# Row maxima one slot and a third ahead instead of two, with a new order of steps and a new prologue rotation

## What is computed

```python
q, k = _rope(q, k)
att = jnp.einsum('bhtd,bhsd->bhts', q, k) / math.sqrt(DH)
att = att + mask                       # causal
w = jax.nn.softmax(att, axis=-1)
y = jnp.einsum('bhts,bhsd->bhtd', w, v)
x = _layernorm(x + y @ W_o)
x = _layernorm(x + ffn(x))             # 8 experts, the best 2 of each token, 256 -> 256
```

## Time and profile before

| | us |
|---|---|
| median of three runs | 3246.15 |
| the profiled execution | 3247.9 |
| its span | 3246.2 |
| PE busy | 3110.3 (96%) |
| VectorE busy | 2684.6 (83%) |
| ACT busy | 1885.3 (58%) |
| GpSimd busy | 1198.2 (37%) |
| first score of attention | at 140.3 |
| the transpositions of x that begin each middle turn | 191.8 apart |
| last turn ends | at 3144.4 |

### The profile page before, as it was taken

How to read it: one execution, slowest core, us unless ns; L and a number is a source line. 1 busy time by engine, 2 the same in 40 slices (tenths; PEclk the granted TensorE clock), 3 DMA queues, 4 the chain that set the end, 5 groups by cost and what they waited for, 6 DMA issues and landing times.

```text
span 3246.2 us, 58552 instructions
## 1 busy us (share of the span) xinstructions
PE 3110.3 (96%) x18752; PEld 1712.3 (53%) x18752; DVE 2684.6 (83%) x8456; ACT 1885.3 (58%) x4257; POOL 1198.2 (37%) x1410
## 2 busy tenths in 40 slices
PE   4789999999999999999999999999999999999987
PEld 2234555555555555555555555555555555555555
DVE  6877888888888888888988888888888888888745
ACT  2266556575565656556575665657565565755551
POOL 3153424444243443424344342434324344442110
PEclk8699999999999999999999999999999999999997
DMA  5344324333442434334333442443443243344000
GB/s 134 62 70 81 60 57 77 62 68 66 80 65 50 78 58 79 60 76 65 55 73 61 83 65 57 73 66 68 66 83 60 55 79 61 69 65 70 4 27 14
DMA packets 174819, 210.95 MB, mean 65 GB/s; under 512 B 26008, under 2 KB 124592, under 8 KB 174256
## 3 DMA queue, kind: packets, MB, share of 16 engines
q1 hardware_dynamic: 173056, 202.98, 35.9%
q10 hardware_dynamic: 1456, 4.23, 0.3%
HBM read 138.44 MB, written 67.11 MB: 63 GB/s over the span
## 4 chain that ended last, share of the span: by engine, by line
PE 84%; DVE 8%; issue 3%; ACT 2%; POOL 1%; DMA 1%; ACTq 0%; SPq 0%; DVEq 0%; POOLq 0%
PE bank L917 22%; PE attend L1012 15%; PE scores L990 14%; PE bank L974 14%; PE bank L954 6%; PE bank L1036 3%; PE bank L963 3%; DVE bank L775 2%; PE bank L1020 1%; PE bank L942 1%; DVE maxima L778 1%; PE bank L1027 1%; PE bank L1044 1%; ACT weights L651 1%; PE bank L1068 1%
## 5 line engine op out<-in xcount | busy, mean ns | idle before, releaser
L651 ACT ACTIVATE weights<-scores 128x512 f32<-128x512 f32 (+3 forms) x3072 | 1333.5, 495 | 886.0 <-PE scores L990 872.7
L775 DVE CUSTOM_DVE_ANT_0 bank<-bank,far_q 128x128 f32<-128x128 f32 (+3 forms) x2048 | 963.1, 512 | 202.7 <-PE bank L974 187.2
L974 PE MATMUL bank<-k_stack,q_stack 96*128 96x512 bf16 (+3 forms) x3072 | 803.6, 333 | 31.7 <-DVE maxima L775 10.5
L990 PE MATMUL scores<-q_stack,k_stack 99*128 99x512 bf16 (+3 forms) x3072 | 821.1, 328 | 10.6 <-ACT weights L651 6.9
L571 POOL TENSOR_SCALAR_AFFINE_SELECT weights<-weights 128x512 f32<-128x512 f32 x512 | 325.4, 637 | 1269.4 <-ACT weights L651 1269.1
L778 DVE TENSOR_REDUCE maxima<-bank 128x1 f32<-128x512 f32 x1024 | 643.9, 682 | 71.2 <-PE bank L974 70.9
L1012 PE MATMUL attend<-weights,values 128*32 128x512 f32 (+3 forms) x6144 | 579.2, 492 | 1.0 <-POOL weights L571 0.9
L990 PEld LDWEIGHTS scores<-q_stack,k_stack 99*128 99x128 bf16 x3072 | 280.1, 97 | 411.8 <-ACT weights L651 154.6
L974 PEld LDWEIGHTS bank<-k_stack,q_stack 96*128 96x128 bf16 x3072 | 276.9, 98 | 400.6 <-issue 153.6
L917 PE MATMUL bank<-wexp_hi,zT_hi 128*128 128x512 f32 x1024 | 381.7, 454 | 11.1 <-DVE lowrows L795 11.1
L891 DVE SCALAR_TENSOR_TENSOR z<-bank,picked,z 128x256 f32<-128x256 f32 x512 | 247.5, 483 | 113.8 <-PE bank L917 104.9
(11 more groups left out here) (110 smaller groups left out, 3133.5 us busy)
## 6 DMA issues: line engine op xcount, KB each, us to landing
parts_scratch<-parts SPq DMA_DIRECT2D x128, 384.0 KB, 2.5
q_stack<-parts_scratch SPq DMA_DIRECT2D x384, 128.0 KB, 7.1
k_stack<-parts_scratch SPq DMA_DIRECT2D x384, 128.0 KB, 7.7
x_in<-in_x SPq DMA_DIRECT2D x64, 256.0 KB, 3.6
z<-in_x SPq DMA_DIRECT2D x32, 512.0 KB, 5.3
out<-z SPq DMA_DIRECT2D x32, 512.0 KB, 3.2
q_stack<-lowrows SPq DMA_DIRECT2D x192, 8.0 KB, 2.4
z<-in_w_exp ACTq DMA_DIRECT2D x1, 1024.0 KB, 4.9
```

The costliest lines, as they stand in the source:

```text
L651: act.activation(weights[:, n % NW, hh, c0:CH], st[(QUAD * n + hh) % NS][:, c0:CH], ACT.Exp, scale=DH ** -0.5).then_inc(S["weights_ready"], 1)
L775: dve.tensor_tensor_reduce(out=b[:, 0:w], in0=b[:, 0:w], in1=far_q[:, CH - w:CH], scale=1.0, scalar=-SENTINEL, op0=ALU.add, op1=ALU.max, a ...
L974: pe.matmul(b[:, 0:w], q_stack[0:ROWS, n, hh, qt * P:(qt + 1) * P], k_stack[0:ROWS, n, hh, kc * CH:kc * CH + w], start=True, stop=True).th ...
L990: pe.matmul(st[(QUAD * n + hh) % NS][:, c0:CH], k_stack[0:MROWS, s, hh, kb * P:(kb + 1) * P], q_stack[0:MROWS, s, hh, qc * CH + c0:(qc + 1 ...
```

## The change

`LATE_B` = 4. In "pre" only the first four items (sixteen steps) of B.1 remain; the other eight items of a slot's maxima are now steps B.3.4 to B.3.11, which run at the beginning of the turn in which they are needed, in "first", "mid" and "last". All 48 rows of the table are written anew, and the segment "pre" too. In "pre" the four halves of heads 0 to 7 (s = 0) are rotated by VectorE alone, which reads the bank in PSUM and writes into a weights buffer, and which does both subtractions; the four of heads 8 to 15 are copied by ACT, shuffled by VectorE and else GpSimd's alone, as in a turn.

```diff
+LATE_B = 4
...
-ST.10.0 ST.10.1 GL.0 ST.10.2 N1A.1 ST.10.3 B.0.11.0 MASK.10 B.0.11.1 B.0.11.2 B.0.11.3 PV.8 PV.9 B.1.0.0 YT.0.0
...
+ST.10.0 ZT.0.0 ZT.0.1 ST.10.1 ST.10.2 ST.10.3 MASK.10 MT.3 QK.0.2 B.0.2.3 B.0.3.0 CAST.0.1.1 ROPE.0.2 PV.8
...
-    if step in (("MC", SLOTS - 1), ("MT", SLOTS - 1)):
-        return seg in ("mid", "last")
+    if step in (("MC", SLOTS - 1), ("MT", SLOTS - 1)) or (kind == "B" and s == SLOTS - 1 and step[2] >= LATE_B):
+        return attend
...
+        cast = [("CAST", *half, n) for half in halves[:4] for n in range(2)]
+        out += [("QK", *halves[0]), ("ROPE", *halves[0]), ("QK", *halves[1]), ("ROPE", *halves[1]), cast[0]]
+        out += [("QK", *halves[2]), ("ROPE", *halves[2]), cast[1], cast[2]]
+        out += [("QK", *halves[3]), ("ROPE", *halves[3]), cast[3], cast[4], ("QK", *halves[4]), ("ROPE", *halves[4])]
+        out += [cast[5], cast[6], cast[7], ("LOAD", 0), ("WSPLIT",)]
+        cast = [("CAST", *half, n) for half in halves[4:] for n in range(2)]
+        out += [*cast[0:2], ("QK", *halves[5]), ("ROPE", *halves[5]), ("VP", 0), ("VP", 1), *cast[2:4], ("LOAD", 1)]
+        out += [("QK", *halves[6]), ("ROPE", *halves[6]), ("VP", 2), ("VP", 3), ("QK", *halves[7])]
+        out += scores[:8] + cast[4:6] + [("ROPE", *halves[7])] + scores[8:16] + cast[6:8] + [("LOAD", 2)] + scores[16:]
+        out += [("MC", 0), ("MT", 0)]
+        out += [("B", 1, it, hh) for it in range(LATE_B) for hh in range(QUAD)]
...
+def on_vector(seg, step):
+
+    return seg == "pre" and step[1] == 0
...
+        def half_of(c, s, k):
+
+            return weights[:, 0, k] if on_vector(c.seg, ("ROPE", s, k)) else rope[:, k % 2]
...
+                elif kind == "ROPE" and on_vector(c.seg, step):
+                    s, k = a
+                    qk, x1, ch = ("QK", s, k), half_of(c, s, k), k // 2
+                    n = bank(c.seg, qk)
+                    if k:
+                        dve.wait_ge(S["rotated"], c.below("rotated", step, 1))
+                        hold()
+                    filled(dve, c, qk)
+                    hold()
+                    dve.stream_shuffle(rope_swap[:, :], bk[n][:, :], SWAP).then_inc(S["swapped"], 1)
+                    dve.tensor_tensor(x1, bk[n][:, :], cos[:, ch * CH:(ch + 1) * CH], ALU.mult).then_inc(free[n], 1)
+                    dve.wait_ge(S["swapped"], c.at("swapped", step))
+                    dve.tensor_tensor(rope_swap[:, :], rope_swap[:, :], sin[:, ch * CH:(ch + 1) * CH], ALU.mult) \
+                       .then_inc(S["sines"], 1)
+                    emptied(dve, c, qk)
+                    hold()
+                    dve.wait_ge(S["sines"], c.at("sines", step))
+                    dve.tensor_tensor(x1, x1, rope_swap[:, :], ALU.add).then_inc(S["rotated"], 1)
```

More of the change, by code:

```diff
@@ L266, in ledger @@
                 add(f"parts_stored{step[2] % 2}", seg, step)
-            if step[0] == "ROPE":
+            if step[0] == "ROPE" and not on_vector(seg, step):
                 add("turning", seg, step)
-                if seg == "pre":
-                    add("sines", seg, step)
-    return book
+            if step[0] == "ROPE" and on_vector(seg, step):
+                add("sines", seg, step)
+    return book
+def on_vector(seg, step):
+    return seg == "pre" and step[1] == 0
 def stack_of(seg, step):
@@ L572, in work @@
                                        pattern=[[0, QUAD], [1, P]], channel_multiplier=-1).then_inc(S["masked"], 1)
-                elif kind == "CAST" and (c.seg != "pre" or a[2]):
+                elif kind == "CAST" and not on_vector(c.seg, step):
+                    if c.seg == "pre" and a[1] == 0:
+                        name = ("rest_ready", "parts_ready")[a[2]]
+                        pool.wait_ge(S[name], c.below(name, step, 1))
+                        pool.sem_inc(S["pool_waits"], 1)
                     rest(pool, c, *a)
@@ L609, in work @@
                                    ACT.Copy).then_inc(fr, 1)
+                elif kind == "QK" and on_vector(c.seg, step):
+                    return
                 elif kind == "QK":
@@ L624, in work @@
                                         c.below(f"parts_stored{k % 2}", ("CAST", s, k, 1), 1, DMA))
[L625 removed]
+                    act.activation(parts[:, k % 2, n], half_of(c, s, k), ACT.Copy).then_inc(S["cast"], 1)
                 elif kind == "VP":
@@ L780, in work @@
                     (s,) = a
-                    emptied(dve, c, ("B", s, ITEMS - 1, QUAD - 1), prev=s == SLOTS - 1 and c.seg != "pre")
+                    emptied(dve, c, ("B", s, ITEMS - 1, QUAD - 1))
                     m = maxima[:, s % 2].rearrange("p (h t) -> p h t", h=QUAD)[:, :, 4:TILES]
@@ L802, in work @@
                     dve.stream_shuffle(rope_swap[:, :], rope[:, k % 2], SWAP).then_inc(S["swapped"], 1)
[L803 to L813 removed]
+                elif kind == "CAST" and on_vector(c.seg, step):
                     rest(dve, c, *a)
```

169 lines of the change are left out of this document (72 added, 97 removed).

## The result

| | before | after |
|---|---|---|
| median of six runs, one chip (us) | 3246.34 | 3258.28 |
| lowest and highest | 3243.84, 3250.74 | 3255.82, 3259.96 |
| profiled execution, its span | 3247.9, 3246.2 | 3256.7, 3255.0 |
| PE busy in the span | 3110.3 | 3126.6 |
| mean granted clock of PE in it | 0.979 | 0.976 |

The ratio is 1.003, 95% interval 1.0019 to 1.0042: slower, by some 10 us. The forecast was 3237, some 9 us faster. The time lies inside the stated range of 3210 to 3264, but the sign is wrong.

The account below looks back on a forecast made before the run. PE was taken to bound the middle turns, busy 2662.7 of 2685.6 us. Prologue -38, first turn 0, 14 turns +22, last turn +8, tail -1 sum to -9: 3238.9 profiled, median 3237, range 3210 to 3264 (8 in 10).

Parts of the forecast that it names:

- The prologue: Ahead of the first score: the first score comes at 102 instead of 140.3 us, gain 38, bounds 28 and 43.
- The seam's wait: Between two turns: x is issued behind MT.2 (transposed maxima), PE waits 2.0 us; +1.5 a turn, bounds +0.5 and +2.7.
- The gate chain: In each turn, transposed logits to gates' transposition: 4.55 us against 4.3 of PE's work, +0.7, bounds 0 and +1.6.
- 14 turns +22: Fourteen turns at +1.6 us each, from the seam, the gate chain and smaller waits, together +22 us.
- tail: Behind the last turn: four of five steps on the same bank as the one before go, -1 us (-2 to +1).
- The first turn: Its 192 maxima are still 192, so 0 us, between -5 and +5.
- The last turn: It takes in 32 maxima that the prologue had: +8 us, PE's price, between 5 and 16.7.
- Rival B: Rows of maxima come late everywhere; a turn costs 3.6 us, total +19, 3265; decides from 2.2 a turn; chance 0.3.

Follow-up runs that it names:

- section 4: The new rotations with the old table of steps and all 48 maxima steps of B.1 ahead of the first score: 0.9944 of the kernel before, median 3231.3 us.
- sections 2 and 3: Section 2, and beside it the changed kernel run again unchanged: 1.0023 of the kernel before, turns mean 194.5 us.
- section 2: The changed kernel with 12 transposes of the identity ahead of PE's wait for x at each seam: 0.996 of the kernel before, median 3238.0 us.
- section 1: The changed kernel with only MT.2 (transposed maxima) moved some 7 us of PE's work earlier: 0.9937 of the kernel before, median 3229.9 us.
- Section 8: New rotations and old order of turns, with 32 maxima steps of slot 1 put off into the first turn alone: 0.9904 of the kernel before, median 3219.8 us.
- section 5: The changed kernel with the gates' transposition and steps behind it 1.5 to 2 us of PE's work later: 1.0054 of the kernel before.
- six transposes in 3: The changed kernel with 6 transposes of the identity ahead of PE's wait for x at each seam: 0.9965 of the kernel before, turns of 193.2 us.

## Why the prediction was wrong

- **The prologue was right.** The load (45.7 for 47.3), the transposed maxima (87.3 for 92.9) and the first score (98.8 for 102) came 1.6 to 5.6 us earlier than worked out, the load's way to its reader was the 15.1 us that it was before, and section 4 shows 17.5 us of the 41 as the rotations' own. The operand in PSUM cost what one in SBUF does, as priced: 0.67 us for the product.
- **The seam's wait was right.** MT.2 to the read of x was taken as 7.2 us against 5.2 of PE's work, 2.0 of wait; the rows give 7.1 (634.38 to 641.50) and 1.94. From its issue to its reader x took 2.92 us (638.58 to 641.50), as in the row before, 2.99. The fit of the Trainium skill (DMA: Bandwidth & Descriptors, Anatomy of one DMA), which gave 0.4 less, is stated there for transfers issued by GpSimd; SP issues x, and the measurement decides.
- **The gate chain** was put at +0.7 and is +0.27. A turn at full clock still takes 193.3, nearly the forecast's 193.4: PE's busy time on the same matmuls is 0.5 us higher (190.63 to 190.16), which made up for it.
- **The step that failed is "14 turns +22".** It priced the 2 us standstill at 2 us. The rows showed PE at clock 0.50 after idling in the prologue and the tail, and I used that clock there, for the transpositions of x, but not for what follows a standstill in the turns. Thirteen turns cost 1.4 us more for it (194.5 against 193.1 with the standstill filled, sections 2 and 3), 18 us in all. In the profiled execution of the changed kernel two of the thirteen had no such stretch and three had one of 6.8 us, and the middle turns cost 36.6, 14.6 over the forecast. Without the low clock they would have cost some 15 (section 2's fourteen take 2700.9 for 2685.4), less than the 22: these turns hold thirteen seams where the sum took fourteen, and the last middle turn is shorter than before. From -9 to +9 lead these 14.6, 4.7 of the first turn, 0.9 and 0.6 of last turn and tail, less 3.0 of the prologue.
- **The first turn** was put at 0, "its 192 maxima are still 192". It grew by 4.7: the seam that ends it has the 2 us wait too, and PE runs 3.4 us at half clock from 148. That stretch stands behind three short waits for VectorE (0.43, 0.62 and 0.59 us within 3 us), not behind the seam's; in section 1's execution it is missing. Section 8 has 32 maxima steps more in that turn for 5.7 us.
- **The last turn** came out right, +8.9 for +8, for another reason: not PE's 8.3 us of added maxima alone, but a wait of 2.4 us for the gates and some 10 us at half clock. In section 1, with the same wait but a full clock, the turn took 163.4, +4.3.
- **Rival B**, the one on the slower side, had the sign but not the mechanism: no rows of maxima came late in the changed kernel. Its threshold, 2.2 us a turn, was passed by x and the clock together. The forecast called itself wrong if a turn grows by over 2.6 us; it grew by 2.6.

Open: why the same standstill lowered the clock at 11 of 14 seams in one execution of the changed kernel and 13 in another, but at one with the gates later (section 5, in the fastest of its six executions), and why the 2.4 us wait of the last turn did so in the changed kernel but not in section 1. Not tried: letting another queue than SP's read x, out of the way of the maxima's rows.

## What to carry to other kernels

Price a new standstill of the bounding engine twice: its length, and what the clock behind it may cost. Here, with PE busy 99% at clock 1.00, a wait of 1.94 us cost 3.3 at most seams; section 5 shows that the second part does not always fall due. And when a prologue gains by a shorter run-ahead, look whether it can be made short once and the steady turns left alone: section 8 keeps 28 of its 37 us, where the change spent more than its 41.

## What the runs showed of the hardware that I had not expected

In the changed kernel a standstill of PE of 1.9 to 2.2 us, in a stretch where it was busy 99% at clock 1.00, was followed at most seams by 3.4 or 6.8 us at a granted clock of 0.50; standstills of 0.2 to 1.2 us, one or two of them at each of 42 seams (sections 1, 2 and six transposes in 3), by none, of 0.9 to 1.14 us ahead of ACT's result by three of fourteen (section 5). Where PE was less busy, in the first turn (86% from 100 to 148), three standstills of 0.4 to 0.6 us went before a stretch at 0.50. Transposes of the identity, which nobody reads, kept the clock up at the seams and made the changed kernel 0.6% faster (section 2). And busy time is no measure of an engine's work then: PE's rose from 3110.3 to 3126.6 us with 18752 matmuls in both.
